# Opening of a fused cross-attention and expert-FFN kernel: norm products and the second tile's scalings moved to GpSimd, two sums of squares moved to VectorE, the zero stores moved behind the weight preparation

## The reference

```python
x = x + attention(layernorm(x), ctx)      # ln, then q, k, v of x and q, k, v of x against ctx
x = x + ffn(layernorm(x))                 # top-2 of 8 experts, and a shared expert

def _div_clamp_fp8(x, scale):             # before the linear layers of q, qx, k and v
    y = clip(x / scale, -448, 448)
    return fp8(bf16(y))
q = _ln(fp8_linear(ln_out, wq), qln_w, qln_b)     # a norm over each head of 128
k = _ln(fp8_linear(ln_out, wk), kln_w, kln_b)
v = fp8_linear(ln_out, wv)
p = softmax(q @ k.T / sqrt(128))          # 16 heads, 8 groups; the same again with ctx for k and v
```

## Time and profile before

| | |
|---|---|
| median of 3 runs | 925.39 us (925.27 to 927.94) |
| the profiled execution | 924.58 us |
| its span in the profile | 922.5 us |
| TensorE busy | 885.3 us (96%) |
| VectorE busy | 740.6 us (80%) |
| ScalarE busy | 673.7 us (73%) |
| GpSimd busy | 497.8 us (54%) |
| DMA | 80.07 MB, mean 87 GB/s |

### The profile page before, as it was taken

One profiled execution on the slowest core, in us unless ns is written; L12 is line 12 of the kernel. 1 busy time (PEld: TensorE's weight loads), 2 busy tenths in 40 slices (PEclk: granted clock), 3 DMA queues, 4 the chain that ended last, 5 costly groups with the idle time before them and its releaser, 6 DMA issues.

```text
span 922.5 us, 22025 instructions
## 1 busy us (share of the span) xinstructions
PE 885.3 (96%) x7812; PEld 594.9 (64%) x7812; DVE 740.6 (80%) x1498; ACT 673.7 (73%) x1182; POOL 497.8 (54%) x509
## 2 busy tenths in 40 slices
PE   5689999999999999999999999999999999999996
PEld 2365667777777777777776776666665565665554
DVE  6789999899999999999999999988699864333332
ACT  6998888888888888888888888885455654444443
POOL 5336766575666775765756666640107632343444
PEclk9989999999999999999999999999999999999999
DMA  9943301001000100110010001031536776888865
GB/s 204 336 120 70 70 25 53 30 31 47 30 30 25 53 30 24 33 45 31 30 47 30 30 25 53 25 121 52 178 121 211 239 196 126 126 139 131 141 103 63
DMA packets 96104, 80.07 MB, mean 87 GB/s; under 512 B 67968, under 2 KB 84096, under 8 KB 95872
## 3 DMA queue, kind: packets, MB, share of 16 engines
q1 hardware_dynamic: 86544, 64.09, 26.0%
q0 software_dynamic: 9456, 14.59, 8.9%
HBM read 50.41 MB, written 18.68 MB: 75 GB/s over the span
## 4 chain that ended last, share of the span: by engine, by line
PE 81%; DVE 11%; ACT 4%; issue 2%; POOL 1%; DMA 0%; POOLq 0%; DVEq 0%; ACTq 0%
PE b_pj L354 25%; PE b_tr L373 9%; PE b_o L414 7%; PE b_sc L385 7%; PE b_acc L457 5%; PE b_pj L1393 5%; PE b_o L1430 5%; PE b_o L1517 3%; PE b_pt L404 3%; PE b_sc L1393 3%; PE b_tr L1393 3%; PE b_pj L1470 2%; PE b_sc L1470 1%; PE b_tr L1470 1%; DVE a L1805 1%
## 5 line engine op out<-in xcount | busy, mean ns | idle before, releaser
L731 POOL TENSOR_TENSOR rstd<-vareps,neghalf 128x4 f32<-128x4 f32 (+1 forms) x128 | 176.2, 1377 | 10.7
L724 POOL TENSOR_SCALAR vareps<-ssq,unit 128x4 f32<-128x4 f32 (+1 forms) x128 | 71.5, 558 | 199.4 <-DVE ssq L543 199.2
L354 PE MATMUL b_pj<-w_hi,xq 128*128 128x512 f16 x384 | 147.7, 385 | 1.1 <-DVE xq L713 0.9
L354 PE MATMUL b_pj<-w_lo,xq 128*128 128x512 f16 x384 | 147.3, 384 | 0.0
L469 ACT ACTIVATE sq<-b_pj 128x512 f32<-128x512 f32 x192 | 115.8, 603 | 40.7 <-PE b_pj L354 39.3
L543 DVE TENSOR_REDUCE ssq<-sq 128x4 f32<-128x512 f32 x192 | 130.5, 680 | 14.1 <-ACT sq L469 12.6
L373 PE MATMUL b_tr<-ident,nrm 128*128 128x128 f32 x768 | 119.6, 278 | 7.5 <-DVE nrm L554 3.2
L1376 POOL DMA_INDIRECT out<-xn x39 | 61.1, 1566 | 109.6 <-ACT xn L1588 46.4
L482 ACT ACTIVATE raw<-b_pj 128x512 f32<-128x512 f32 x192 | 117.5, 612 | 0.0
L373 PEld LDWEIGHTS b_tr<-ident,nrm 128*128 128x128 f32 x768 | 90.1, 141 | 38.4 <-issue 6.7
L502 ACT ACTIVATE qT<-b_tr,col,hw 128x512 f32<-128x512 f32 x128 | 100.8, 787 | 1.5 <-PE b_tr L373 1.5
(11 more groups left out here) (329 smaller groups left out, 2028.5 us busy)
## 6 DMA issues: line engine op xcount, KB each, us to landing
nst<-in_ffw SPq DMA_DIRECT2D x40, 512.0 KB, 3.3
wload<-in_ffw SPq DMA_DIRECT2D x20, 512.0 KB
xbuf<-zero SPq DMA_DIRECT2D x13, 387.0 KB, 9.6
x_sb<-in_x SPq DMA_DIRECT2D x4, 512.0 KB, 14.1
wproj<-in_ctxT SPq DMA_DIRECT2D x1, 2048.0 KB, 10.8
xhl<-in_w_all SPq DMA_DIRECT2D x4, 512.0 KB, 18.8
wproj<-in_wprojT POOLq DMA_DIRECT2D x4, 512.0 KB, 5.3
rowbuf<-xr SPq DMA_DIRECT2D x16, 128.0 KB, 1.8
```

The costliest lines, as they stand in the source:

```text
L354: last = pe.matmul(o, x, w[kind][:, k, at:at + BANK], start=(k == 0 and n_ == 0), stop=(k == KT - 1 and n_ == len(terms) - 1))
L731: pool.tensor_tensor(rstd[:, r % 2, c, :], vareps[:, r % 2, c, :], neghalf[:, 0:1].unsqueeze(2).to_broadcast(shape), ALU.pow)\
```

## The change

- For the steps N = 0, 1, 2 (`EARLY = 3`), the second and third norm product are done by GpSimd, right after the inverse roots of the step, and counted in a new semaphore `norm_pool`. From step 3 on they stay on VectorE. `after_norm` picks the semaphore and the count for those that wait.
- Tile 1 is scaled by GpSimd in two halves, at the start of slot -2, instead of in four parts on ScalarE; VectorE clips and rounds it at once instead of in four parts. Tile 0 stays as it was.
- `squares(0)` and `squares(1)` of the context move from ScalarE to VectorE, behind the second tile's quantization and behind the second unit of a later group.
- On the SP queue the wait for `wc_done` of 32 now stands ahead of the 13 zero stores, so that these, too, go out after the last unit of weights; the loads of `nst` follow behind them.

```diff
+            EARLY = 3
+            def after_norm(eng, N, c):
+                if 0 <= N < EARLY:
+                    eng.wait_ge(s["norm_pool"], 2 * N + c)
+                elif N >= EARLY:
+                    eng.wait_ge(s["norm_done"], 2 * (N - EARLY) + c)
@@ attention_sync
                 sp.wait_ge(s["zero_set"], 2)
+                sp.wait_ge(s["wc_done"], 8 * 4)
                 for a in range(0, ET, TURN - 1):
                     b = min(a + TURN - 1, ET)
                     sp.dma_start(x_rows[:, a:b, :], zero[:, 0:b - a, :].bitcast(U32)).then_inc(s["xbuf_zero"], 16)
-                sp.wait_ge(s["wc_done"], 8 * 4)
                 for n in range(NPC):
                     after(sp, "wsq_done", n)
                     sp.dma_start(nst[:, :], ffw[n, :, :]).then_inc(s["nst_in"], 16)
@@ dve_norm
+                    if N < EARLY:
+                        return
@@ dve_quantize
-                if t >= 2 and part != 2:
+                if t >= 1 and part != 2:
                     return
-                j = slice(0, 4) if t >= 2 else PARTS[part]
+                j = slice(0, 4) if t >= 1 else PARTS[part]
@@ pool_rstd
+                    if q and N < EARLY:
+                        pool.wait_ge(s["rs_done"], 2 * N + 2)
+                        for c in range(1, NN):
+                            pool.wait_ge(s["raw_done"], 4 * N + c + 1)
+                            after(pool, "t_done", NN * (N - 1) + c + 1)
+                            pool.tensor_tensor(nrm[:, c, :].rearrange("p (a b) -> p a b", b=D),
+                                               raw[:, r % 2, c, :].rearrange("p (a b) -> p a b", b=D),
+                                               wide(rstd[:, r % 2, c, :], D), ALU.mult).then_inc(s["norm_pool"], 1)
@@ attention_scalar
                 def squares(n):
+                    if n < 2:
+                        return
-                    (-3, "token"): lambda: (act_token_scaled(act, 0, 3), act_token(act, 1, 0), act_token_scaled(act, 1, 0)),
+                    (-3, "token"): lambda: (act_token_scaled(act, 0, 3), act_token(act, 1, 0)),
-                    (-2, "raw 2"): lambda: (high(2, 2), high(2, 3), act_token_scaled(act, 1, 1), act_token_scaled(act, 1, 2)),
+                    (-2, "raw 2"): lambda: (high(2, 2), high(2, 3)),
-                    (-1, "raw 2"): lambda: act_token_scaled(act, 1, 3),
@@ attention_vector
+                def squares(n):
+                    sq16 = ctxh[:, :, :, :].rearrange("p t k c -> p (t k c)").bitcast(BF16)[:, n * HC * H:(n + 1) * HC * H]
+                    src = cstage[:, n * HC * H:(n + 1) * HC * H]
+                    dve.wait_ge(s["ctx_in"], 16)
+                    dve.scalar_tensor_tensor(sq16, src, 1.0, src, ALU.mult, ALU.mult, accum_out=sqsum[:, n:n + 1])\
+                        .then_inc(s["wsq4_done"], 1)
-                    (-2, "max"): lambda: dve_quantize(dve, 1, 0),
-                    (-2, "residual"): lambda: (dve_quantize(dve, 1, 1), dve_quantize(dve, 1, 2)),
+                    (-2, "residual"): lambda: (dve_quantize(dve, 1, 2), squares(0)),
-                    (-1, "max"): lambda: low(3, 3),
+                    (-1, "max"): lambda: (low(3, 3), squares(1)),
-                    (-1, "stats"): lambda: (low(2, 0), dve_quantize(dve, 1, 3)),
+                    (-1, "stats"): lambda: low(2, 0),
@@ attention_gpsimd
-                          {1: lambda: (token_rstd(1), output_weights(0)), ...
+                          {-2: lambda: (pool_token_scaled(pool, 1, 1), pool_token_scaled(pool, 1, 2)),
+                           1: lambda: (token_rstd(1), output_weights(0)), ...
```

More of the change, by code:

```diff
@@ L126, in build @@
         cout = sb("cout", [P, 1], F32, attn)
-        names = ("share_set aT_done aTh_done aTl_done wst_in1 wst_in0 w16_in0 "
+        names = ("share_set aT_done aTh_done aTl_done norm_pool wst_in1 wst_in0 w16_in0 "
                  "w16_in1 w16_in2 w16_in3 w32_in0 w32_in1 w32_in2 w32_in3 mats16 wproj_in0 wproj_in1 wproj_in2 wproj_in3 v16_in0 v16_in1 v16_in2 v16_in3 ctxl_done sum_ones cols_in wc_done consts ctx_in "
@@ L266, in place16 @@
                 return w16[n], "w16_in%d" % n, 32
+            EARLY = 3
[4 more added lines that the diff above has]
+                    eng.wait_ge(s["norm_done"], 2 * (N - EARLY) + c)
             def scaled(t):
-                return 4 * t if t < 2 else t + 6
+                return 4 * t if t < 1 else t + 3
             def scaled_halves(t):
-                return 4 * t if t < 2 else 2 * t + 4
+                return 4 * t if t < 1 else 2 * t + 2
             def wide(ap, n):
@@ L340, in step @@
                         terms = ((j, w_hi), (j, w_lo))
[L341 to L345, removed]
+                    if i == 0 and r == 0 and c in (0, 1, 3):
+                        pe.wait_ge(s["xq_done"], (1, 2, 0, 3)[c])
+                    if i == 0 and r == 2 and c == 1:
+                        pe.wait_ge(s["xq_done"], 4)
+                    if i >= 1 and r == 0 and c == 0:
                         pe.wait_ge(s["xq_done"], scaled(i) + 1)
@@ L364, in step @@
                     else:
-                        pe.wait_ge(s["norm_done"], 2 * N + c)
+                        after_norm(pe, N, c)
                     after(pe, "tev_done", m)
@@ L480, in step @@
                         else:
-                            after(act, "norm_done", 2 * N - 4 + c)
+                            after_norm(act, N - 2, c)
                         act.activation(raw[:, r % 2, c, :], bk, ACT.Copy).then_inc(s["raw_done"], 1)
@@ L702, in dve_quantize @@
             def dve_quantize(dve, t, part):
-                if t >= 2 and part != 2:
+                if t >= 1 and part != 2:
                     return
-                j = slice(0, 4) if t >= 2 else PARTS[part]
-                M = scaled(t) if t >= 2 else 4 * t + part
+                j = slice(0, 4) if t >= 1 else PARTS[part]
+                M = scaled(t) if t >= 1 else part
                 dst = xq_all[:, ring(t), :, j, :]
-                dve.wait_ge(s["y_done"], scaled_halves(t) + 2 if t >= 2 else M + 1)
+                dve.wait_ge(s["y_done"], scaled_halves(t) + 2 if t >= 1 else M + 1)
                 dve.tensor_scalar(dst, y16[:, :, j, :], FP8_MAX * DOWN, -FP8_MAX * DOWN, ALU.min, ALU.max)\
@@ L727, in step @@
                     if q:
-                        after(pool, "norm_done", 2 * N - 2)
+                        after_norm(pool, N - 2, 2)
                     else:
@@ L1144, in attention_gpsimd @@
                 run_slots(pool, [(3, pool_rstd(0)), (PREP, pool_token_scaled), (3, pool_rstd(1)), (ROWS, pool_rows)],
[L1145 removed]
+                          {-2: lambda: (pool_token_scaled(pool, 1, 1), pool_token_scaled(pool, 1, 2)),
+                           1: lambda: (token_rstd(1), output_weights(0)), 2: lambda: output_weights(1), 3: lambda: output_weights(2), 4: lambda: (output_weights(3), token_rstd(2), token_rstd(3))}, {})
         attn.close()
```

1 line of the change is left out of this document (removed).

## The result

| | before | after |
|---|---|---|
| median | 925.33 us (4 runs, 924.42 to 927.94) | 940.21 us (4 runs, 938.5 to 944.21) |
| ratio | | 1.0162, 95% interval 1.0139 to 1.0186 |
| the profiled execution | 924.58 us | 944.21 us |
| its span in the profile | 922.5 us | 942.1 us |
| mean granted TensorE clock | 0.995 | 0.985 |

The change is slower by 14.9 us. The forecast was slower by 5.6, with 936 as the upper end of the range: right in direction, far off in size.

The account below looks back on a forecast made before the run. Bounds: ScalarE (20 to 40 us), TensorE (54 to 66), VectorE (66 to 102), then TensorE. Piece 0 lands at 86.2, VectorE's stage is 5.8 us later with the 3.0 gain inside: 925.39 + 5.8 = 931.2, called 931; range 925 to 936.

Parts of the forecast that it names:

- ScalarE waits for piece 0, behind the stores in the SP queue: Piece 0's load queues behind thirteen zero stores; ScalarE, there at 75.8, waits 10 us for it to land at 86.2.
- The rival by which the stores hold nobody up: Stores drain as issued or piece 0's load passes them; only the gain is left: 922.4 us, chance 0.13.
- With it at 62.3: First zero store goes out at 62.3 us, the last weight unit being done 3.0 earlier than 65.28.
- g: Gain ahead of the scales: 3.0 us, between 0 and 3.85, from work taken off ScalarE less waits for GpSimd.
- VectorE isn't the bound: Up to the scales, VectorE's added sums and removed norm products balance at about nothing; it is busy 14.71 of 20.
- the TensorE stage behind passes it on: The TensorE stage behind the scales, 54 to 66 us, passes on the gain of 3.0 us.
- the 0.85 that I had allowed: About 0.85 taken off ScalarE's 3.85 us, for GpSimd's step 1 norm products falling on VectorE's quantization and first sum of squares.
- Stores 17.3, then 3.3 and 3.3: From 62.3: stores 17.3 us at 289 GB/s, piece 0's load 3.3, one shared weight transfer 3.3; it lands at 86.2.
- The rival with both transfers in the sum: Stores share with both weight transfers, 3.3 more: piece 0 lands at 89.5, kernel 934.5 us, chance 0.17.
- my range let the stores go faster, 320: Unshared case at its best: stores at 320 GB/s, gain 3.85, piece lands at 80.4; 925.4 us, within no change, chance 0.20.
- The sum can start 3.46 after the piece lands: VectorE's sum starts 3.46 us after piece 0 lands (2.83 plus 0.63 for the exponentials), at 89.7 instead of 83.88.
- All of VectorE's stage is then as much later, and the TensorE stage too: VectorE, with 0.7 us idle in 36, can't catch up; its stage and the TensorE stage behind come 5.8 us later.

Follow-up runs that it names:

- with the stores back: Changed kernel with the wait for the last weight unit put back behind the zero stores, so these run from 20 us again: 923.73 us, ratio 0.9975.
- the clock kept up: Changed kernel plus 56 matmuls that nobody reads, keeping TensorE at work while ScalarE waits for piece 0: 940.3 us, ratio 1.0162 to the kernel before.
- light weights: Changed kernel with the first two output projection weight loads bringing one block of eight, used eight times: 937.66 us, ratio 1.0123 to the kernel before.

## Why the prediction was right and wrong

**ScalarE waits for piece 0, behind the stores in the SP queue: right.** The wait, its place, what ends it and who stands behind it are as forecast, and the runs show it from both sides: with the moved wait alone 942.19, with the load ahead of the stores 923.73. The rival by which the stores hold nobody up falls.

**"With it at 62.3" (g = 3.0): too large by 2.1.** The stores went out at 64.38. Two steps failed. First, "VectorE isn't the bound": with ScalarE's 3.85 us removed, the norm products kept on VectorE and the two sums added to it, the scales began 0.16 earlier. Taking the norm products off VectorE is what brings the gain; that this is because the engines alternate through three banks is my reading, not tested apart. Second, "the TensorE stage behind passes it on": with the stores back the scales began 3.76 earlier (48.88), nearly all of the 3.85, and the last unit was done only 2.31 earlier (62.97), since the chain between them ran through TensorE.

How large g is scatters, too. Seven profiles have the opening of the change, and in them the last unit was done between 62.96 and 64.91, so g was 0.4 to 2.3; all are below 3.0. The first profile of the changed kernel lost 1.0 us at 22.64, where VectorE waited 1.36 for a high half; in the second the same instruction came at 21.59 after a wait of 0.32, and g was 1.85 (63.43).

GpSimd does hold VectorE, but I looked for that in the quantization and the sums of squares only. For the first sum that was so; VectorE of the changed kernel, and GpSimd beside it:

```profile
38.26 2.06 DVE L1002 SCALAR_TENSOR_TENSOR ctxh<-wproj 128x1024 bf16<-128x1024 f32 x1
...
42.17 1.21 DVE L1002 SCALAR_TENSOR_TENSOR ctxh<-wproj 128x1024 bf16<-128x1024 f32 x1
...
38.01 3.22 POOL L756 TENSOR_TENSOR nrm<-raw,rstd 128x512 f32<-128x512 f32 x2
```

It took 2.06 us instead of the second's 1.21, the 0.85 that I had allowed, and GpSimd's pair, which took 2.07 at 50 us in the version with the stores back, 3.22: each waited for the other once. The 1.44 in the chain of the scales I had not looked for. In both profiles of the changed kernel the chain of waits runs through the held instructions, but without them the last unit is done only some 0.25 us earlier, since TensorE is then what it waits for.

"SBUF — State Buffer" of the Trainium skill, section on the two separate sides, gives the lock to whichever starts first, for the whole instruction, against VectorE instructions with two SBUF inputs or in a two-port mode. The trace agrees: the first sum, `npow` and `unit` were held to the end of a GpSimd product, and the reciprocal between them took its 0.18 beside one. I had applied the rule to the long instructions alone; nothing in it depends on length.

**"Stores 17.3, then 3.3 and 3.3": too small by 4.5.** It was 28.44 instead of 23.9. The bytes were 5.15 MB for the stores (387 KB are 396 thousand bytes, I took 387), 0.52 for the piece and 1.05 for two weight transfers, 6.7 MB instead of 6.1, and the mean rate was 237 GB/s, not the 289 of 38 to 52 us: 6.73 / 0.237 = 28.4. In the four other profiles with the stall it was 225 to 232. The rival with both transfers in the sum, which a rule of the Trainium skill supported ("DMA: Bandwidth & Descriptors", Queues, rings and completion order: the DMA engines take turns between queues, packet by packet), was right on the sharing: the landing of a weight transfer went from 5.5 us in the kernel before (64 to 95 us) to 10.4. The trace agrees on the sharing; the turns packet by packet no run shows. But sharing was not what I had too small: both transfers together cost 3.3 to 4.8 us, and 3.3 were in the sum. The missing 4.5 are the rate, nearly all of them. With next to no weights to share with, stores and piece took 25.14 us, where 17.3 + 3.3 = 20.6 were forecast. I had given the rate no lower end at all; my range let the stores go faster, 320, and never slower. Why it was lower stays open.

**"The sum can start 3.46 after the piece lands": right**, 3.34 (92.82 to 96.16).

**"All of VectorE's stage is then as much later, and the TensorE stage too": too small by 2.9.** The sum is 12.28 late and the mark 15.17. I had counted as a saving the 1.6 us by which VectorE, before, came later to its sum than ScalarE would have allowed. But the way out of the stall doesn't lead through this sum. The chain of waits of the changed kernel, 93 to 98 us:

```profile
93.97 0.68 ACT kT L510
94.65 0.14 issue
94.78 1.09 PE b_tr L381 x4
95.87 2.01 PE b_o L422 x16
97.88 1.82 PE b_pj L362 x4
```

It goes from ScalarE's eviction of the keys straight to TensorE, and the eviction is late by the whole delay of the square. With the clock kept up, the time from square to mark is that of before within 0.03 us, so the delay passes in full. The halved clock, 1.2 GHz from 84 to 100 us, adds the other 1.2 in this profile.

**The sum put right:** square late by 2.1 + 4.5 more than forecast (86.2 + 6.6 = 92.8), which is 13.98 behind 78.84; plus 1.2 for the clock; 15.2 us at the mark, 940 for the whole. Forecast: 5.8.

**The range** ended at 936 because it took both transfers and a g of 1.5, but no slower rate, no way around VectorE's sum and no halved clock beside them. All of them came at once.

## What to carry to other kernels

In a queue that works in order, ask for each transfer that is moved what small load then stands behind it, and when it is wanted; split the large transfers around that load, or leave them where they were. For the landing, count all bytes of all queues in that time, and leave room below the rate that the trace shows for full DMA engines: the lowest window shown from before had 283 GB/s, and 225 to 237 came. When work goes to GpSimd, lay its instructions over VectorE's chains in time: one of instructions on three numbers lost 1.44 us there, a sum over 128x1024 only 0.85. Then ask what else the next stage waits for: of the 1.44 some 0.25 counted. And take a gain of one or two us from several profiles, not from one.

## What the runs showed that I had not expected

- With the DMA engines full (share 1.01 to 1.10), rows of some 1 KB moved at 314 GB/s from 66 to 72 us in the changed kernel, at 289 from 38 to 52 before, and at 232 over 25 us in the kernel with light weights. That they are stores in all three is plain, why the rate differs is not; it was not tried apart.
- VectorE instructions on three numbers and on one took 0.89 and 0.86 us instead of 0.17 and 0.13, each to the end of a GpSimd norm product of 128x512; that this cost the last unit of weights only some 0.25 us was no less of a surprise.
- A sum of squares with a running sum over 128x1024 takes VectorE 1.21 us when not held, and 0.08 for the readout, a little more than ScalarE's 1.04.
- An idle TensorE (14.75 us ahead of 94.78) and some sixteen us of halved clock cost only 1.2 us behind the stall in the first profile and 0.4 in the second. Ten of these sixteen, 84 to 94, had no work for TensorE.
- After a stall of 14 us nothing is caught up: 66.5 us from the square to the mark without it, and the same with it and the clock kept up.
